# A graph-network kernel: layer 1's wide groups rotate over three row slots, not four

## The chip, the cores and the metric

The kernel runs on one core of one Trainium2 chip. The metric is the device time of one execution in microseconds (us), lower is better. The kernel before took 3185.05 us, the median of three runs (3184.51, 3185.05 and 3190.93).

## What is computed

Two layers of message passing over one graph of 12,500 nodes with 128 float32 features and 212,500 edges, which come sorted by target node (`dst`). The reference, cut to what matters:

```python
def layer0(x, weight, w_comp, h_bias, src, dst, etypes):
    W = einsum('rb,bio->rio', w_comp, weight)      # 16 relations from 8 bases
    h = einsum('ni,rio->rno', x, W)
    return segment_sum(h[etypes, src], dst, 12500) + h_bias
def layer1(feat, W_neigh, W_self, b_self, src, dst):
    deg = maximum(segment_sum(ones, dst, 12500), 1)
    agg = segment_sum(feat[src], dst, 12500)
    return feat @ W_self + b_self + (agg / deg[:, None]) @ W_neigh
x = layernorm(x + layer0(x, ...))                  # called x1 below
x = layernorm(x + layer1(x, ...))
```

The code counts the same two as 1 and 2 (its names are `w1`, `n1` and `w2`, `n2`); "layer 1" below is the first of them, as in the change's title.

## The kernel before, in words

**Tiling.** The edges are cut into chunks of 128, eight chunks (`CPG`) make a group, and there are 208 groups. The last one, 207, has five real chunks. For each chunk GpSimd issues one indirect DMA (L1640, L1644, L1671) which fetches the 128 source rows into one eighth of a slot of the tile `rows`; TensorE multiplies them with a one-hot matrix, and VectorE adds the small result to the target nodes' columns of `acc`.

**Layer 1.** The first 20 groups (`PLAIN`) are narrow: a row is x alone, 512 bytes, and `rows` holds them in eight slots (`SLOTS`), slot g % 8. From group 20 on they are wide: a row of the table `x_x_rows` is x and, beside it, x1 of the same node where that has been laid there already, or zeros, 1024 bytes. A wide slot takes the room of two narrow ones, so `rows` has room for four, and group g uses wide slot g % `WIDE_SLOTS`. For each group TensorE makes layer 1's sums (`sum_half`, L2257), then, from the same slot, layer 2's sums of the sources whose x1 was there (`early_half`, L2269). Its last matmul raises `rows_read`, so `rows_read` is n + 1 when group 20 + n has been read for good.

**Nodes finish as the edges go by.** Every 4.25 groups, one part of 256 nodes (49 parts) is complete: TensorE projects a run of groups (`project`, L2297), VectorE adds (L1909), ScalarE stages (L1701), TensorE transposes (L2225), VectorE and ScalarE normalise, and SyncE stores x1 (L1531 to the wide table for the first 44 parts, counted by `laid1`; L1533 to `x1_rows`, counted by `stored1`).

**What sets the order on GpSimd.** Its program (L1617 to L1674) is one hand-written list. Before group g's gathers it waits until the group that last used the slot has been read: L1621 for narrow groups, L1623 to L1628 for wide ones. Before a half of a wide group it also waits for the table parts that the half may read (L1637). After the last group of layer 1 come the two held groups of layer 2 (`HELD`, j = 0 and 1), whose edges had been left over from narrow groups 18 and 19. They go to narrow slots 0 and 1, that is to wide slot 0, and wait at L1651 for the last group that used wide slot 0, and for parts 45 and 46 to be stored (L1653). Group j = 2 and all behind it read any row of x1 and so wait for the stores of the last two parts (L1662). Then come layer 2's remaining groups, each after the read of the group eight before it (L1663). The lines around the two waits:

```python
1623                            s = g % WIDE_SLOTS
1624                            before = [e for e in range(g) if (e % SLOTS // 2 if narrow(e) else e % WIDE_SLOTS) == s][-1]
...
1628                                pool.wait_ge(rows_read, before - PLAIN + 1)
...
1649                        if j < HELD:
1651                            pool.wait_ge(rows_read, max(e for e in range(groups) if e % WIDE_SLOTS == j // 2) - PLAIN + 1)
...
1660                        if j == HELD:
1661                            for k in (last_part - 1, last_part):
1662                                pool.wait_ge(stored1[k % 2], stores(k))
```

TensorE ends layer 1 with group 207, a projection of that group and the transpose of the last part, and begins layer 2 with `total_late(0)` (L2324) and the sums of j = 0 (L2372). From j = 20 on layer 2's sums are L2379.

Of the kernel before, what the change touches and what calls it, by code (L numbers as in the profile page):

```python
# [31 lines left out]
CPG = 8  # L32
UNROLL = 8
SLOTS = 8
AHEAD = 6
WIDE_SLOTS = 4
TPH = 4
QUAD = TPH * P
SHIFT = 3 * QUAD
# [18 lines left out]
def gnn_kernel(nc, x_in, src, dst, etype, weight, w_comp, h_bias, w_neigh, w_self, b_self, x1_rows, out):  # L58
# [118 lines left out]
    with ctx:  # L177
        def sb(name, shape, dt=F32):
            return ctx.enter_context(nc.sbuf_tensor(name, shape, dt))
# [6 lines left out]
        def sem(name):  # L186
# [8 lines left out]
        xout = sb("xout", [P, 2, TPH, d])  # L195
        rows = sb("rows", [P, SLOTS, CPG, d])
        wide_rows = rows[:, :, :, :].rearrange("p s c f -> p (s c f)").rearrange(
            "p (s c f) -> p s c f", s=WIDE_SLOTS, c=CPG)
        idx = sb("idx", [P, SLOTS, CPG], I32)
        src_t = sb("src_t", [P, chunks + SLOTS * CPG], I32)  # L200
        rel_t = sb("rel_t", [P, chunks])
# [1000 lines left out]
        with nc.If(in_order):  # L1202
# [102 lines left out]
            def narrow(g):  # L1305
                return g < PLAIN

            def slot_rows(g, c):
                return rows[:, g % SLOTS, c, :] if narrow(g) else wide_rows[:, g % WIDE_SLOTS, c, 0:d]

# [150 lines left out]
            with nc.Block(no_gpsimd_drain=True) as block:  # L1461
# [156 lines left out]
                def _(pool):  # L1618
                    for g in range(AHEAD, groups):
                        if narrow(g):  # L1620
                            after(pool, w1.z_done, g - SLOTS + 1)  # L1621
                        else:
                            s = g % WIDE_SLOTS  # L1623
                            before = [e for e in range(g) if (e % SLOTS // 2 if narrow(e) else e % WIDE_SLOTS) == s][-1]
                            if narrow(before):
# [7 lines left out]
                        for c in range(real):  # L1633
# [9 lines left out]
                            else:  # L1643
                                gather = pool.indirect_dma_start(  # L1644
                                    out=wide_rows[:, g % WIDE_SLOTS, c, :], out_offset=None, in_=table,
                                    in_offset=bass.IndirectOffsetOnAxis(ap=src_t[:, k:k + 1], axis=0))
                            gather.then_inc(w1.gathered[g % SLOTS][c // HALF], signal_of(range(real), c))
                    for j in range(late_groups):
                        if j < HELD:
                            pool.wait_ge(held_marked, 1)  # L1650
                            pool.wait_ge(rows_read, max(e for e in range(groups) if e % WIDE_SLOTS == j // 2) - PLAIN + 1)  # L1651
                            for k in (settled - 2, settled - 1):
# [1047 lines left out]
```

## Time and profile before

| | |
|---|---|
| median of three runs | 3185.05 us |
| lowest, highest | 3184.51, 3190.93 us |
| the profiled execution's own time | 3189.88 us |
| its span in the trace | 3188.5 us |
| mean granted TensorE clock | 0.649 |
| indirect DMAs of rows in layer 1 (wide) | 1501 |
| indirect DMAs of rows in layer 2 (held, then all others) | 16, then 839 |

Busy time counts an engine's own instructions. Register, branch and semaphore instructions are not in it. For an indirect DMA the busy time on POOL (GpSimd) is that of issuing it; the landing comes later. Behind a row stands the engine's idle time ahead of it, and what ended that: "issue" where nothing that the profile shows was waited for.

### The profile page before, as it was taken

To read this page: it belongs to the slowest core of one execution; us is meant where nothing else is said; L and a number is where in the kernel's file an instruction comes from. 1 tells how busy PE (TensorE), PEld (TensorE's weight loads), DVE (VectorE), ACT (ScalarE), POOL (GpSimd) and SP (SyncE) were. 2 spreads that over 40 slices of the span, in tenths; PEclk is the share of its full clock that TensorE was granted. 3 is DMA by queue.
4 is the path that set the end of the run, shared out by engine and by line. 5 is a ranking of instruction groups with operands and counts; after the bars stand their busy time and mean duration, and the time that the engine had idled before them with its cause. 6 is when DMAs were issued, how large, how long until landed. Compare 5 with 4: busy or idle time off the path is not lost. (4 is left out here: it accounts for less than half of the span.)

```text
span 3188.5 us, 36471 instructions
## 1 busy us (share of the span) xinstructions
PE 2287.2 (72%) x11654; PEld 2071.9 (65%) x11654; DVE 1557.9 (49%) x4527; ACT 334.1 (10%) x668; POOL 2391.8 (75%) x2528
## 2 busy tenths in 40 slices
PE   2678888888888888888888888864555555555455
PEld 1567777777777778887777887854444444444444
DVE  6453343334333333344333333346677777777345
ACT  2111111111111111111111111100000000000011
POOL 7777777777777777777777777777777777777775
PEclk9876666676666665567666666665565556566576
DMA  4944444444444344444444444332222222222323
GB/s 117 330 129 122 121 121 121 116 122 121 122 125 122 115 122 120 120 120 122 126 120 118 120 122 120 112 83 53 63 68 68 63 63 70 67 73 70 92 80 79
DMA packets 257565, 345.54 MB, mean 108 GB/s; under 512 B 47072, under 2 KB 190021, under 8 KB 257366
## 3 DMA queue, kind: packets, MB, share of 16 engines
q0 software_dynamic: 104528, 263.42, 29.7%
q1 hardware_dynamic: 127398, 66.86, 7.2%
q10 hardware_dynamic: 25440, 12.85, 1.3%
q8 instruction: 95, 1.56, 0.2%
q14 instruction: 104, 0.85, 0.1%
HBM read 311.40 MB, written 44.38 MB: 112 GB/s over the span
## 5 line engine op out<-in xcount | busy, mean ns | idle before, releaser
L1644 POOL DMA_INDIRECT rows<-x_x_rows,src_t x1501 | 1425.3, 950 | 459.7 <-issue 455.7
L2257 PE MATMUL zps<-acc,rows 128*128 128x168 f32 x3322 | 833.0, 415 | 206.5 <-DMA rows<-x_x_rows,src_t 188.4
L2257 PEld LDWEIGHTS zps<-acc,rows 128*128 128x128 f32 x3322 | 715.2, 266 | 238.6 <-DMA rows<-x_x_rows,src_t 122.4
L1671 POOL DMA_INDIRECT rows<-x_rows,picked_mem x695 | 657.6, 946 | 211.8 <-issue 211.5
L2379 PE MATMUL zps<-acc,rows 128*128 128x128 f32 x1390 | 323.2, 406 | 406.9 <-DMA rows<-x_rows,picked_mem 394.0
L2269 PEld LDWEIGHTS yps<-oh,rows 128*128 128x128 f32 x3002 | 579.0, 278 | 0.0
L2379 PEld LDWEIGHTS zps<-acc,rows 128*128 128x128 f32 x1390 | 278.8, 298 | 441.9 <-DMA rows<-x_rows,picked_mem 273.8
L2269 PE MATMUL yps<-oh,rows 128*128 128x21 f32 x3002 | 537.1, 322 | 0.0
L1896 DVE TENSOR_TENSOR acc<-acc,yps 128x42 f32 (+1 forms) x831 | 163.1, 196 | 592.4 <-PE yps L2277 460.4
L1909 DVE TENSOR_TENSOR acc<-acc,tps 128x21 f32 x831 | 146.9, 177 | 540.2 <-PE tps L2297 379.3
L2297 PE MATMUL tps<-acc,picked_mem 128*128 128x336 f32 (+3 forms) x816 | 340.8, 585 | 27.5 <-ACT acc L1723 27.5
L1870 DVE TENSOR_TENSOR acc<-oh,tps 128x1344 f32<-128x1344 f32 x208 | 323.2, 1554 | 29.3 <-PE tps L2244 1.8
L1723 ACT COPY acc<-zps 128x672 f32<-128x672 f32 x208 | 148.4, 714 | 1399.4 <-PE zps L2257 1380.6
L2297 PEld LDWEIGHTS tps<-acc,picked_mem 128*128 128x128 f32 x816 | 199.0, 254 | 146.7 <-issue 90.5
L2109 DVE TENSOR_TENSOR acc<-place_b,tps 128x1024 bf16<-128x1024 bf16 x190 | 230.1, 1211 | 0.0
L2023 DVE TENSOR_TENSOR acc<-acc,zps 128x128 f32 (+1 forms) x448 | 119.9, 268 | 224.7 <-PE zps L2379 139.7
L1671 POOL DMA_INDIRECT rows<-x_rows,src_t x144 | 136.6, 948 | 49.1 <-issue 43.6
L2244 PE MATMUL tps<-wc_blk,acc 128*128 128x64 f32 x416 | 88.8, 386 | 73.3 <-DVE acc L1870 61.4
L2244 PEld LDWEIGHTS tps<-wc_blk,acc 128*128 128x128 f32 x416 | 83.9, 296 | 79.3 <-DVE acc L1870 64.7
L2372 PE MATMUL zps<-oh,rows 128*128 128x21 f32 x320 | 73.8, 380 | 85.5 <-DMA rows<-x_rows,src_t 85.5
L1640 POOL DMA_INDIRECT rows<-in_x_dram,src_t x112 | 107.3, 958 | 34.1 <-issue 33.8
L2372 PEld LDWEIGHTS zps<-oh,rows 128*128 128x128 f32 x320 | 70.2, 325 | 89.7 <-DMA rows<-x_rows,src_t 53.4
(295 smaller groups left out, 1527.6 us busy)
## 6 DMA issues: line engine op xcount, KB each, us to landing
rows<-x_x_rows,src_t POOLq DMA_INDIRECT x1501, 2.7
erep<-in_edge_type_dram SPq DMA_DIRECT2D x207, 64.0 KB
x_x_rows<-zrow ACTq DMA_DIRECT2D x20, 576.0 KB, 3.6
x_x_rows<-in_x_dram SPq DMA_DIRECT2D x20, 576.0 KB
rows<-x_rows,picked_mem POOLq DMA_INDIRECT x695, 2.5
x_rows<-xout SPq DMA_DIRECT2D x49, 128.0 KB
xin<-in_x_dram SPq DMA_DIRECT2D x48, 128.0 KB
out_dram<-xout SPq DMA_DIRECT2D x24, 256.0 KB, 2.4
```

Of the source, the lines that this page charges most:

```text
L1644: gather = pool.indirect_dma_start(out=wide_rows[:, g % WIDE_SLOTS, c, :], out_offset=None, in_=table, in_offset=bass.IndirectOffsetOnAxis ...
L1671: pool.indirect_dma_start(out=rows[:, j % SLOTS, c, :], out_offset=None, in_=x1_rows[0:n_nodes, :], in_offset=bass.IndirectOffsetOnAxis(ap ...
L1723: nc.scalar.copy(zsb[:, kept_at(g)].rearrange("p (h w) b n -> p h (w b n)", h=2), zduos[g % 2]).then_inc(w1.z_copied, 1)
L1870: nc.vector.tensor_tensor(a[:, g % 4], oh1[:, g % 6].unsqueeze(2).to_broadcast([P, CPG, n_bases, SPAN]), wcp[:, m % 2, g % HALF, :].rearra ...
L1896: add = nc.vector.tensor_tensor(target, target, windows_of(g)[:, first:2, c, :], ALU.add)
L1909: add = nc.vector.tensor_tensor(target, target, ybank1[:, y0:y0 + SPAN], ALU.add)
L2109: nc.vector.tensor_tensor(to_lane[:, t % UNROLL], place_b[:, 0, at].unsqueeze(2).to_broadcast([P, CPG, P]), lanes_p.unsqueeze(1).to_broadc ...
L2244: last = nc.tensor.matmul(wcp[:, m % 2, q, :], eoh[:, m % 2, q, :], wc_blk[:, :, :].rearrange("p c b -> p (c b)"), start=True, stop=True)
L2257: last = nc.tensor.matmul(zwins[g % 2][:, c // HALF, c % HALF // 2], slot_rows(g, c), a[:, g % 4, c], start=(c % 2 == 0), stop=(c % 2 == 1 ...
L2269: last = nc.tensor.matmul(windows_of(g)[:, 0, c // 2], wide_rows[:, g % WIDE_SLOTS, c, d:2 * d], oh1[:, g % 6, c], start=(c % 2 == 0), sto ...
L2297: last = nc.tensor.matmul(ybank1[:, y0:y0 + duos * SPAN].rearrange("p (w n) -> p w n", n=SPAN), wb[:, b, :], kept[:, 0:duos, b, :], start= ...
L2379: last = nc.tensor.matmul(sums_of(j, c0, P), rows[:, j % SLOTS, c, :], oh2[:, j % 4, c, :], start=(c == c0), stop=(c == c0 + n - 1))
```

## The change

`WIDE_SLOTS` goes from 4 to 3. The view `wide_rows` keeps its cut into four wide slots (`SLOTS // 2`), of which the fourth is no longer used. All places that take a wide slot or the group before it in that slot (L1309, L1623, L1624, L1645, L1651, L2270) follow the constant. So a wide group waits for the group three before it, not four; group 20 waits for narrow group 13, not 17; and the last group in wide slot 0, for which the held groups wait at L1651, is 207 (207 % 3 = 0), where it was 204 (204 % 4 = 0).

```diff
-WIDE_SLOTS = 4
+WIDE_SLOTS = 3
...
         wide_rows = rows[:, :, :, :].rearrange("p s c f -> p (s c f)").rearrange(
-            "p (s c f) -> p s c f", s=WIDE_SLOTS, c=CPG)
+            "p (s c f) -> p s c f", s=SLOTS // 2, c=CPG)
```

## Rows read from the trace of the kernel before

**Rows 1.** The page's busy times: engine, us, share of the span, instructions

```profile
PE 2287.2 (72%) x11654; PEld 2071.9 (65%) x11654; DVE 1557.9 (49%) x4527; ACT 334.1 (10%) x668; POOL 2391.8 (75%) x2528
```

**Rows 2.** Who POOL waited for, whole span: us in total, times, longest us

```profile
POOL rows L1644 <- issue: 455.7, 1496, 0.3
POOL rows L1671 <- issue: 255.1, 837, 0.3
...
POOL rows L1671 <- DMA x_rows<-xout: 5.5, 1, 5.5
...
POOL rows L1644 <- DMA x_x_rows<-xout: 3.4, 3, 1.8
...
POOL rows L1644 <- PE yps L2269: 0.6, 2, 0.3
```

**Rows 3.** Who PE waited for, 2118 to 3168 us (layer 2)

```profile
PE zps L2379 <- DMA rows<-x_rows,picked_mem: 388.5, 149, 6.2
PE zps L2372 <- DMA rows<-x_rows,src_t: 85.5, 33, 3.5
```

**Rows 4.** The chain that ended last, its first long piece: start, us, what

```profile
3167.39 4.97 DMA rows<-x_rows,picked_mem
```

**Rows 5.** Timeline of POOL, middle of layer 1: start, us, instruction [idle before, releaser]

```profile
1338.99 0.94 POOL L1644 DMA_INDIRECT rows<-x_x_rows,src_t  x1 [1.75 <-DMA x_x_rows<-xout]
1343.98 0.95 POOL L1644 DMA_INDIRECT rows<-x_x_rows,src_t  x1 [0.30 <-PE yps L2269]
...
1384.06 0.95 POOL L1644 DMA_INDIRECT rows<-x_x_rows,src_t  x1 [0.30 <-issue]
```

**Rows 6.** Timeline of PE, middle of layer 1

```profile
1334.27 1.74 PE L2269 MATMUL yps<-oh,rows 128*128 128x21 f32 x8
...
1375.23 1.74 PE L2269 MATMUL yps<-oh,rows 128*128 128x21 f32 x8
```

**Rows 7.** Timeline of POOL, end of layer 1 and start of layer 2

```profile
2067.34 0.95 POOL L1644 DMA_INDIRECT rows<-x_x_rows,src_t  x1 [0.30 <-issue]
...
2092.33 0.95 POOL L1644 DMA_INDIRECT rows<-x_x_rows,src_t  x1 [0.30 <-issue]
2093.58 0.94 POOL L1655 DMA_INDIRECT rows<-x_rows,held_idx  x1 [0.30 <-issue]
...
2112.31 0.94 POOL L1655 DMA_INDIRECT rows<-x_rows,held_idx  x1 [0.31 <-issue]
2118.79 0.94 POOL L1671 DMA_INDIRECT rows<-x_rows,src_t  x1 [5.54 <-DMA x_rows<-xout]
```

**Rows 8.** Timeline of PE, end of layer 1 and start of layer 2

```profile
2061.33 1.74 PE L2269 MATMUL yps<-oh,rows 128*128 128x21 f32 x8
...
2099.94 4.24 PE L2297 MATMUL tps<-acc,picked_mem 128*128 128x168 f32 x16 [5.56 <-ACT acc L1723]
...
2105.96 0.53 PE L2257 MATMUL zps<-acc,rows 128*128 128x168 f32 x2
2106.33 0.29 PE L2269 MATMUL yps<-oh,rows 128*128 128x21 f32 x2
...
2112.38 0.69 PE L2225 MATMUL tps<-ident,stage 128*128 128x128 f32 x2 [3.08 <-ACT stage L1701]
2121.63 0.35 PE L2324 MATMUL yps<-ones_b,late_b 128*112 128x128 bf16 x1 [8.56 <-DVE base_f L2033]
```

**Rows 9.** Timeline of SyncE's issues, same stretch

```profile
2116.19 0.40 SPq L1533 DMA_DIRECT2D x_rows<-xout  x1
```

**Rows 10.** Lines L1644, L1655 and L1671: durations ns min/median/max, first and last start

```profile
L1644 POOL DMA_INDIRECT rows<-x_x_rows,src_t x1501: 940/946/1182, 208.6 to 2092.3; - x188
DMA to landing us min/median/max: 2.7/2.7/3.7
...
L1655 POOL DMA_INDIRECT rows<-x_rows,held_idx x16: 940/944/947, 2093.6 to 2112.3; - x16
...
L1671 POOL DMA_INDIRECT rows<-x_rows,src_t x144: 938/944/1447, 2118.8 to 2298.0; - x144
```

## The prediction, made before the changed kernel was run

> **What bounds the kernel now.** I read the engines' busy times first. POOL is the busiest at 2391.8 us, but that is only 75% of the span, and PE at 72% stands close behind [rows 1]. The shares leave the bound open, so I went on to what POOL waited for. Its idle time is nearly all "issue", 0.3 us before each indirect DMA: 1496 of layer 1's 1501 wide gathers, and 837 of layer 2's 839 [rows 2]. A gather costs 0.946 us plus those 0.30 us [rows 2, 10], 1.25 us from start to start, a group of eight 10 us. Real waits are few: 3.4 us for table parts in layer 1 and 5.5 us once, at the switch to layer 2 [rows 2]. From the first wide gather at 208.6 us to the end POOL issues almost without a break, and PE waits for its rows in layer 2: 388.5 us in 149 waits at L2379, 85.5 us in 33 at L2372 [rows 3]. The chain that ended last has as its first long piece the last gather on its way, from 3167.39 us for 4.97 us [rows 4]. So POOL's list of gathers bounds the kernel, in both layers. A new stall on POOL ahead of layer 2's gathers moves the end by its whole length; a later PE, DVE or ACT does nothing until POOL waits for it.
>
> The change adds no instruction and takes none away. It changes for which group POOL waits, in three places.
>
> **1. Into the wide groups.** Group 20 waits for group 13, not 17; groups 21 and 22 wait for 17 and 19, earlier groups than PE's newest. These waits are no tighter than the old ones, so they can't cost; and they can't gain more than the 0.6 us in two waits that is all L1644 ever waited for PE, each no longer than the usual 0.3 [rows 2]. Worth 0.
>
> **2. The steady rotation.** Group g now waits until PE has read g - 3. I compare POOL's first gather of g with the end of PE's L2269 of g - 3 in the unchanged timeline; while that difference stays above zero the new wait is already over. Near the end, group 205 starts at 2067.34 us and PE has read 202 at 2061.33 + 1.74 = 2063.07, a slack of 4.3 us [rows 7, 8]. That is the smallest of the 185 differences. In the middle PE falls behind too: group 133 starts at 1343.98, group 130 is read at 1334.27 + 1.74 = 1336.01, slack 8.0; group 137 at 1384.06 against 1375.23 + 1.74 = 1376.97, slack 7.1 [rows 5, 6]. In that same episode POOL already idles 1.75 us, 1.45 above the usual 0.30, for a table part (the gather at 1338.99 us [rows 5]). That wait comes from the same late PE and binds with 7 to 8 us of slot slack left, so in the middle it holds POOL back before a three-slot wait does. At the end no table part is waited for any more (the last of the 44 is asked for in group 191), and the 4.3 us are unguarded. Worth 0 here; if PE is some us later in another execution a slot wait appears. At the end that costs nothing either, by step 3: there PE's own end sets the time. I keep 0 to +3 us (two waits like the 1.45 above).
>
> What hides the removed slot is thus PE's distance of under three groups. The Trainium skill ("Trainium Kernel Development and Optimization", Best Practices) says to double-buffer so that DMA and compute overlap; by it three slots are one more than needed and the sum would be 0, no change. The trace agrees for the rotation, by the 4.3 us. It isn't all the change does.
>
> **3. The held groups.** This is the step that I expect to cost. Before, the 16 held gathers wait for group 204 and follow the last gather of 207 without a pause: 2092.33, then 2093.58, with 0.30 us of "issue" [rows 7]. Now wide slot 0 is last used by group 207 itself, of which the last rows have only just been asked for. PE has read 207 at 2106.33 + 0.29 = 2106.62 us [rows 8]; that is 13 us behind POOL, since PE is catching up and loses 5.56 us to a late copy of ACT before the projection at 2099.94 [rows 8]. So:
> - First held gather: 2106.62 + 0.30 = 2106.9 us, against 2093.58. POOL stands for 13.3 us.
> - The 16 gathers take (2112.31 - 2093.58) / 15 = 1.249 us each, 20.0 us in all [rows 7]. Next one possible: 2126.9 us.
> - Before, the gathers were done at 2112.31 + 0.94 = 2113.25, and POOL then idled 5.54 us for the store of the last part, so j = 2 began at 2118.79 [rows 7]. That store is issued at 2116.19 [rows 9] and hangs on PE, ACT and DVE behind group 207 (the transpose at 2112.38 [rows 8]), none of which waits for a held gather. It is then over before 2126.9 and costs nothing.
> - Loss: 2126.9 - 2118.79 = **8.1 us**. Of the 13.3 us, 5.2 are paid out of the old wait (5.54 less the 0.30 of issue).
>
> It hardly depends on when PE ends. If PE reads 207 later or earlier by a few us, old and new start of j = 2 both move with it, as the old one is set by the store 12.17 us after that read (2118.79 - 2106.62). Only once the store would be in time for the end of the old gathers (read of 207 before 2106.62 - 5.24 = 2101.4 us) does the loss shrink by 1 us per us. Lower end: rows of the last gather land 2.7 us after 2092.33 [rows 10], PE needs 0.53 + 0.29 us for them [rows 8], so the read ends at 2095.9 at the earliest, j = 2 starts at 2095.9 + 0.3 + 20.0 = 2116.2 against 2113.6: +2.6 us. Upper end: +8.1, and one long gather of step 4, 8.6.
>
> **4. Behind it.** Nobody waits for held rows early: PE takes up j = 0 only after 2121.63, where it had been waiting 8.56 us for DVE's L2033 [rows 8]. j = 0 is landed by then, j = 1 some us later; PE then follows POOL as before. The moved gathers now run at 2107 to 2127 us, beside other DVE work. In the old place they took 940 to 947 ns each, and the 144 gathers that come next, beside the DVE work of layer 2's start, have the same median, 944 ns, with a longest of 1447 [rows 10]. So I take 0, and 0.5 us, one such gather, as the bound; a gain is excluded, as the shortest is 938.
>
> **Sum.** 0 + 0 + 8.1 + 0: the profiled execution, 3189.88 us (span 3188.5 and 1.4 around it), would become 3198.0. It is itself 4.8 us above the median of 3185.05, and nothing in the loss hangs on that difference, so I put the 8.1 on the median: 3193.1 us, +0.25%.
>
> **Rivals.**
> - *PE isn't late at the end* (the mildest case of step 3). If PE reads 207 before 2099.6 us, the loss is under 6.3 us; at the floor it is 2.6 and the time 3187.6, under 0.2% and not to be told from no change. For it: the clock differs between executions. Against it: PE's late end is mostly ACT's late copy and the projection behind it, 2099.94 + 4.24, which don't go away with the clock. 9%.
> - *No stall that counts, not slower*. The mechanism: POOL's 13.3 us stand but layer 2 catches up, because its pace is set by PE or DVE and POOL had run ahead into its eight slots. Price 0, time 3185.1. It decides if PE's lag there exceeds the 8.1 us. Against it: 182 waits of PE for rows, 474 us [rows 3], and no wait of POOL for a slot in layer 2 [rows 2]. It is also what the rule on double buffering gives. 7%.
> - *Slot waits in layer 1 as well*. PE's lag differs by execution, and the slack of 4.3 or 7.1 us runs out in the middle of the layer. Two or three waits of 1 to 1.8 us (the table's wait is the nearest row [rows 5]) add 3 to 5 us: 3196 to 3198. 9%.
> - *The change doesn't act*, because some index still counts four slots: every use takes the constant, and the view alone keeps four. 1%.
>
> **The numbers.** The forecast, 3193.1, has 74%. A measurement of this kernel can tell 0.2%, 6.4 us, from no change; the three runs of before spread over as much. The range goes from the floor of step 3, 3185.05 + 2.6 = 3187.6, to the highest run with the loss, 3190.93 + 8.1 = 3199.0. Slower by over 0.2%: the forecast and the slot waits, 83%, less about 10 for a scatter that hides 8.1 under 6.4, 73%. Within 0.2%: the mild case, the catching up and no action, 17%, and most of that 10, less what scatters out: 25%. Faster: 2%, scatter alone, as nothing on POOL's path gets earlier.
>
> **What would show it.** In the changed profile: POOL's first L1655 with an idle time of about 13 us ended by PE's L2269, 16 gathers in 20 us, then L1671 at once with 0.30 of issue in place of 5.54 for the store; layer 2 from there on as long as before, 1048.6 us from its first L1671 to its last; layer 1's L1644 with the same few waits as before, all 1501 within 1884 us. I'd be wrong if L1644 showed waits for L2269 of more than 0.3 us (step 2), if L1671 still waited for the store (step 3), or if layer 2's stretch came out shorter (step 4).

## The result, and the profile after

The changed kernel takes **3193.26 us** (median of 14 runs, 3191.35 to 3200.51) where the kernel before takes 3185.86 us (median of 14 runs, 3182.78 to 3192.57 and one of 3232.99). The ratio is 1.0023, 95% interval 1.0015 to 1.0031: slower by 7.4 us. The forecast was 3193.1.

The page's busy times are those of before [rows 1] to within 10 us:

```profile
PE 2277.4 (71%) x11654; PEld 2063.7 (65%) x11654; DVE 1557.7 (49%) x4527; ACT 334.1 (10%) x668; POOL 2392.7 (75%) x2528
```

Who POOL waited for in the changed kernel, whole span (in all, times, longest us):

```profile
POOL rows L1644 <- issue: 456.0, 1497, 0.3
POOL rows L1671 <- issue: 255.4, 838, 0.3
...
POOL rows L1655 <- issue: 12.4, 16, 7.8
POOL rows L1644 <- DMA x_x_rows<-xout: 3.9, 4, 1.4
```

Against [rows 2] one entry is new and one is gone. L1655, the held gathers, now has one idle stretch of 7.8 us; L1671's wait of 5.5 us for the store is no longer there. L1644 has no wait for L2269 at all, so the rotation over three slots never held POOL up.

The timeline of POOL at the switch of layers, which answers to [rows 7]:

```profile
2093.81 0.95 POOL L1644 DMA_INDIRECT rows<-x_x_rows,src_t  x1 [0.30 <-issue]
2102.56 0.94 POOL L1655 DMA_INDIRECT rows<-x_rows,held_idx  x1 [7.80 <-issue]
...
2121.30 0.94 POOL L1655 DMA_INDIRECT rows<-x_rows,held_idx  x1 [0.30 <-issue]
2122.55 0.95 POOL L1671 DMA_INDIRECT rows<-x_rows,src_t  x1 [0.30 <-issue]
```

PE, which answers to [rows 8]:

```profile
2095.20 4.13 PE L2297 MATMUL tps<-acc,picked_mem 128*128 128x168 f32 x16 [2.13 <-ACT acc L1723]
...
2101.49 0.29 PE L2269 MATMUL yps<-oh,rows 128*128 128x21 f32 x2
```

and SyncE, which answers to [rows 9]:

```profile
2111.35 0.40 SPq L1533 DMA_DIRECT2D x_rows<-xout  x1
```

PE has read group 207 at 2101.49 + 0.29 = 2101.78 us, and POOL starts the held gathers 0.78 us later. The profile calls the idle time "issue" and names no releaser. That it is the wait of L1651 for group 207 is read from the program and from this distance; the experiments below put the wait in and take it out by itself. The store of the last part, on which j = 2 hung before, is issued at 2111.35 and by the 2.6 us of before (2116.19 to 2118.79 [rows 7, 9]) would let POOL go at 2113.95. It is long over at 2122.55.

**Where the time went.** From the last wide gather to the first of j = 2 it is 28.74 us (2093.81 to 2122.55), against 26.46 in the profiled execution of before [rows 7]. Those 26.46 hold 5.24 us of waiting for the store: 17 gathers in a row take only 17 x 1.249 = 21.2 us. With the changed kernel's own PE and store the old wait would have given 21.2 us, j = 2 at 2115.0, later than the 2113.95 of the store. So the change costs 7.5 us in this execution. The profiled executions lie only 3.7 us apart (3188.5 and 3192.2 in span), as that of before was 4.0 us above the median of its 14 runs and that of the changed kernel 0.4 above its own. Without its 5.24 us of waiting for the store the profiled execution of before would have taken 3184.64 us, which is near that median. It fits that most executions of before have no such wait, but none of them was traced.

### The profile page after: what moved, and what is told of

It is laid out like the page before. It is cut to its first block, busy times and chain, and to the rows that moved or that the text cites. A ratio compares the mean times of both kernels' runs of the same rounds, so it can differ in the third digit from the quotient of the medians.

```text
span 3192.2 us, 36471 instructions
## 1 busy us (share of the span) xinstructions
PE 2277.4 (71%) x11654; PEld 2063.7 (65%) x11654; DVE 1557.7 (49%) x4527; ACT 334.1 (10%) x668; POOL 2392.7 (75%) x2528
## 4 chain that ended last, share of the span: by engine, by line
POOL 70%; issue 23%; PE 4%; DVE 1%; DMA 1%; DVEq 0%; ACT 0%; POOLq 0%; ACTq 0%; SPq 0%
POOL rows L1644 41%; POOL rows L1671 24%; POOL rows L1640 3%; PE zps L2257 2%; POOL rows L563 1%; PE tps L2297 1%; PE yps L2269 1%; POOL rows L1655 0%; DVE acc L1909 0%; PE zps L2379 0%; PE tps L2244 0%; DMA rows<-x_rows,picked_mem 0%; DVE acc L1870 0%; DMA rows<-x_x_rows,src_t 0%; DVEq L1909 0%
## 5 line engine op out<-in xcount | busy, mean ns | idle before, releaser
L1644 POOL DMA_INDIRECT rows<-x_x_rows,src_t x1501 | 1426.0, 950 | 459.9 <-issue 456.0
L1671 POOL DMA_INDIRECT rows<-x_rows,picked_mem x695 | 657.3, 946 | 211.8 <-issue 211.5
L2379 PE MATMUL zps<-acc,rows 128*128 128x128 f32 x1390 | 326.3, 409 | 398.8 <-DMA rows<-x_rows,picked_mem 377.4
L2269 PEld LDWEIGHTS yps<-oh,rows 128*128 128x128 f32 x3002 | 570.2, 274 | 0.0
L2379 PEld LDWEIGHTS zps<-acc,rows 128*128 128x128 f32 x1390 | 282.2, 301 | 433.7 <-DMA rows<-x_rows,picked_mem 277.1
L2269 PE MATMUL yps<-oh,rows 128*128 128x21 f32 x3002 | 528.4, 319 | 0.0
L2297 PE MATMUL tps<-acc,picked_mem 128*128 128x336 f32 (+3 forms) x816 | 331.2, 572 | 24.2 <-ACT acc L1723 24.1
L1671 POOL DMA_INDIRECT rows<-x_rows,src_t x144 | 136.4, 947 | 43.9 <-issue 43.9
L2372 PE MATMUL zps<-oh,rows 128*128 128x21 f32 x320 | 75.0, 383 | 91.6 <-DMA rows<-x_rows,src_t 89.5
L2372 PEld LDWEIGHTS zps<-oh,rows 128*128 128x128 f32 x320 | 71.1, 328 | 96.2 <-DMA rows<-x_rows,src_t 54.9
```

Of the source, the lines that this page charges most:

```text
L1644: gather = pool.indirect_dma_start(out=wide_rows[:, g % WIDE_SLOTS, c, :], out_offset=None, in_=table, in_offset=bass.IndirectOffsetOnAxis ...
L1671: pool.indirect_dma_start(out=rows[:, j % SLOTS, c, :], out_offset=None, in_=x1_rows[0:n_nodes, :], in_offset=bass.IndirectOffsetOnAxis(ap ...
L2269: last = nc.tensor.matmul(windows_of(g)[:, 0, c // 2], wide_rows[:, g % WIDE_SLOTS, c, d:2 * d], oh1[:, g % 6, c], start=(c % 2 == 0), sto ...
L2297: last = nc.tensor.matmul(ybank1[:, y0:y0 + duos * SPAN].rearrange("p (w n) -> p w n", n=SPAN), wb[:, b, :], kept[:, 0:duos, b, :], start= ...
L2379: last = nc.tensor.matmul(sums_of(j, c0, P), rows[:, j % SLOTS, c, :], oh2[:, j % 4, c, :], start=(c == c0), stop=(c == c0 + n - 1))
```

## The experiments

Three theories were set against each other. A: all the loss is the held groups' wait, and the rotation is free. B: the shorter rotation itself costs. C: layer 2 makes a delay good. Seven kernels were run, three of them more than once, since something unforeseen turned up: on the chips of the first eight (numbers 9 and 3) the kernel before takes 4364 us, on that of the last four (number 0) 3185 to 3188 us, like the runs of the result. Each ratio is against the kernel before on the same chip. The expectations call 9 and 3 the slow chips. I take chip 0 first, which is like that of the result.

### The held groups without the wait, three slots

Layer 2's groups are moved round by six narrow slots, so the held ones land in narrow slots 6 and 7, which three wide slots leave free, and L1651 is dropped:

```diff
+HELD_AT = 6
...
-                            pool.wait_ge(rows_read, max(e for e in range(groups) if e % WIDE_SLOTS == j // 2) - PLAIN + 1)
...
-                                    out=rows[:, j, c, :], out_offset=None, in_=x1_rows[0:settled * PART, :],
+                                    out=rows[:, (j + HELD_AT) % SLOTS, c, :], out_offset=None, in_=x1_rows[0:settled * PART, :],
...
-                                out=rows[:, j % SLOTS, c, :], out_offset=None, in_=x1_rows[0:n_nodes, :],
+                                out=rows[:, (j + HELD_AT) % SLOTS, c, :], out_offset=None, in_=x1_rows[0:n_nodes, :],
```

(and the same index in L2372 and L2379).

> Three wide slots, the held groups in narrow slots 6 and 7 without a wait for rows_read, a third time, in the hope of a chip on which before takes 3185 us, as in the last two runs. There my theory (all the loss is the held groups' wait) gives the time of before, within 3 us; the rival (the rotation over three slots costs) gives +7 us, as in the changed kernel. On a slow chip it says nothing new: 3975 us.

Measured: 3185.22 us (12 runs) against 3187.64 (22 runs), ratio 0.9993 (0.9984 to 1.0003). The same as before. The new constant moves the lines down by one, so its wide gathers are L1645. POOL at the switch:

```profile
2094.94 0.95 POOL L1645 DMA_INDIRECT rows<-x_x_rows,src_t  x1 [0.30 <-issue]
2096.19 0.94 POOL L1655 DMA_INDIRECT rows<-x_rows,held_idx  x1 [0.30 <-issue]
...
2114.92 0.94 POOL L1655 DMA_INDIRECT rows<-x_rows,held_idx  x1 [0.30 <-issue]
2116.16 0.94 POOL L1671 DMA_INDIRECT rows<-x_rows,src_t  x1 [0.30 <-issue]
```

2094.94 to 2116.16 is 21.2 us, the bare 17 gathers. And what L1645 waited for in this kernel:

```profile
  issue: 454.8, 1493
  DMA x_x_rows<-xout: 6.6, 5
  PE yps L2269: 0.9, 3
```

Three waits named PE, of 0.3 us each, which is the usual gap. The five waits for table parts hold 5.1 us above it, against 2.5 in three before [rows 2]; they are no slot waits. B falls on this chip: three slots without the held wait cost nothing.

### The held wait alone, four slots

```diff
-                            pool.wait_ge(rows_read, max(e for e in range(groups) if e % WIDE_SLOTS == j // 2) - PLAIN + 1)
+                            pool.wait_ge(rows_read, groups - PLAIN)
```

> Four wide slots, the held groups wait for group 207 to be read, a third time. Where before takes 3185 us my theory gives +7 to +8 us, with POOL idle 7 to 14 us before the first held gather and 0.30 us before j = 2; the rival gives 0. On a slow chip: 4370 us again.

Measured: 3194.85 us (11 runs) against 3187.64, ratio 1.0027 (1.0018 to 1.0035), 7.2 us more. The wait alone makes all of the change's loss. POOL and, behind it, PE at the switch:

```profile
2090.53 0.94 POOL L1644 DMA_INDIRECT rows<-x_x_rows,src_t  x1 [0.30 <-issue]
2101.20 0.94 POOL L1655 DMA_INDIRECT rows<-x_rows,held_idx  x1 [9.73 <-issue]
...
2121.18 0.94 POOL L1671 DMA_INDIRECT rows<-x_rows,src_t  x1 [0.30 <-issue]
```

```profile
2100.13 0.29 PE L2269 MATMUL yps<-oh,rows 128*128 128x21 f32 x2
```

From the read of 207 (2100.42 us) to the first held gather it is 0.78 us again, and 19.98 us more to j = 2.

### A lead of two groups

Four slots, and POOL waits in addition until PE has read g - 2:

```diff
                                 pool.wait_ge(rows_read, before - PLAIN + 1)
+                            if g - 2 >= PLAIN:
+                                pool.wait_ge(rows_read, g - 2 - PLAIN + 1)
```

> Four wide slots as in the kernel before, with one wait more: a wide group g also waits until PE has read g - 2. Only POOL's lead over PE is that of two slots; the slots, the addresses and the held groups' wait are those of before. On the chips of the first eight runs (before 4364 us, PE's slow stretches): if the gain of fewer slots there comes from the shorter lead, about 3820 us, as with two slots. If it comes from where the rows lie, 4364 us. Where before takes 3185 us: 4 to 16 us more than before, from waits for L2269 while PE lags.

Measured on chip 0: 3202.01 us (4 runs) against 3185.29 (7 runs), ratio 1.0052 (1.0035 to 1.0069), 16.7 us more, just over my range of 4 to 16. What its wide gathers (L1646 here, by the two lines added) waited for:

```profile
L1646 POOL DMA_INDIRECT rows<-x_x_rows,src_t x1501: 940/946/1201, 209.2 to 2108.9; - x188
its engine sat idle before it (us, times) until:
  issue: 446.7, 1456
  PE yps L2271: 29.1, 45
```

The 45 waits for PE make 29.1 us, 15.6 above the usual 0.3 each; only ten of them are longer than 0.8 us. Layer 1's gathers take 1899.7 us, where those of before take 1883.7 [rows 10]. So the edge lies between three and two: a lead of three groups is free, one of two costs 16 us. The smallest slack over three slots, 4.3 us [rows 7, 8], says so beforehand: with one group of 10 us less it would be -5.7.

### A pause at each group

Four slots, and POOL waits before each wide group for its own last gathers to land:

```diff
+                        if g > PLAIN:
+                            for h in range(2):
+                                pool.wait_ge(w1.gathered[(g - 1) % SLOTS][h], ((g - 1) // SLOTS + 1) * 16 * HALF)
```

> Four wide slots and the full lead of four groups, but POOL waits before each wide group until its own last group of gathers has landed, a pause of about 2 us a group that doesn't depend on PE. On the slow chips PE's slow stretches end 3 to 6 us after POOL stops issuing. If POOL's unbroken issue is what keeps PE slow, regular pauses of 2 us shorten the stretches and the kernel gets faster than before's 4364 us, to 3850 to 4150, in spite of 187 pauses. If only the lead over PE counts, PE stays as slow and the pauses are lost or swallowed: 4350 to 4700 us. Where before takes 3185 us: about 187 x 1.7 = 320 us more than before.

It ran on chip 0, so it only shows the price there: 3629.88 us (4 runs), ratio 1.1393 (1.1374 to 1.1412), 444.6 us more, against 320 that I had expected. Its wide gathers waited:

```profile
  DMA rows<-x_x_rows,src_t: 483.2, 186
```

2.60 us each, 2.30 above the usual, and not the 1.7 that I had put. 187 x 2.3 = 430. The time rises by all of POOL's stalls again, and by some 15 us more. What it was made for, chips 9 and 3, stayed untried.

### The same kernels on chips 9 and 3

The changed kernel itself:

> The changed kernel itself, beside variants that part its two effects. The first four variants ran on a chip (number 9 in the results) where the kernel before takes 4363.8 us, not 3185, and where PE stood still for about 1 ms in all with nothing that it waited for. Where before takes about 3185 us again, I expect +7 to +8 us for this kernel. Where before takes about 4360 us again, the variants with fewer slots were 9 and 12% faster there, so I expect this one 8 to 9% faster.

3976.14 us (6 runs) against 4364.82 (17 runs), ratio 0.9125 (0.9089 to 0.9162). There it is **faster by 389 us**.

The two kernels that part A and B, each run on chip 9 and again on chip 3:

> Three wide slots as in the change, but layer 2's groups are moved round by six narrow slots, so the held groups land in narrow slots 6 and 7, which no wide group uses now, and their wait for rows_read falls away. My theory (the loss is all in the held groups' wait, the rotation over three is free): as the kernel before, within 0.1%; POOL's last wide gather is followed by the first held one after 0.30 us. Rival (the shorter rotation itself costs, by slot waits in layer 1): it stays slower by about 7 us, as the changed kernel, and L1644 shows waits for PE's L2269 well over 0.3 us.

> Three wide slots, the held groups in narrow slots 6 and 7 and without a wait for rows_read, a second time. Where before takes about 3185 us: my theory gives no difference to before (within 0.1%), the rival, that the shorter rotation costs, gives +7 us as in the changed kernel. On the slow chip: as a1_changed less 8 us at most.

3979.32 us against 4363.77, ratio 0.9125 (0.9101 to 0.9150), and 3972.38 against 4364.82, ratio 0.9117 (0.9080 to 0.9155). Not the time of before, as I had expected of the first, but within 4 us that of the changed kernel.

> Four wide slots as before, and only the held groups' wait is that of the change: for group 207 to be read. My theory: +7 to +8 us against the kernel before, as the changed kernel, with one idle stretch of 7 to 13 us on POOL before the first held gather and none before layer 2's j = 2. Rival (the rotation costs): within 2 us of the kernel before.

> Four wide slots, the held groups wait for group 207 to be read, a second time. Where before takes about 3185 us: my theory gives +7 to +8 us, the rival 0. On the slow chip it was +5 us of 4364, inside the scatter, and I expect that again.

4369.22 us, ratio 1.0018 (0.9996 to 1.0041), and 4375.86, ratio 1.0032 (1.0005 to 1.0059): 5 and 11 us more, of runs that scatter over 40 to 50. The first had been expected 7 to 8 us slower; on these chips so small a loss can't be told from none.

Two wide slots and the free held groups (`WIDE_SLOTS = 2`):

> The kernel e1_held_free with two wide slots, so a wide group waits for the group two before it, and the held groups wait for none. In the trace of before, 21 of 186 groups would start up to 5.7 us too early for that, in three stretches where PE lags (groups 60 to 72, 128 to 141, 196 to 207). My theory: real waits for L2269 appear in those stretches alone, a few us each time a stretch begins, less of them once POOL has fallen back; layer 1's last wide gather comes 8 to 20 us later and the time rises by 4 to 16 us, as the last stretch is free. Rival (POOL's lead over PE is only needed where it has one, PE's lag is made good): under 3 us.

> Two wide slots and the held groups free of the wait, a second time. Where before takes about 3185 us: real waits for L2269 in the stretches where PE lags, layer 1's last wide gather 8 to 20 us later, the time up by 4 to 16 us; the rival says under 3 us. On the slow chip: 12% faster again.

3827.25 us, ratio 0.8778 (0.8754 to 0.8802), and 3818.84, ratio 0.8755 (0.8725 to 0.8784). Faster still, by 12%, where I had expected 4 to 16 us more of the first. It wasn't run on chip 0; by the lead of two above I estimate that it would lose some 16 us there.

Eight more gathers in layer 2, whose rows nothing reads:

```diff
+                        if j == 3:
+                            for c in range(CPG):
+                                pool.indirect_dma_start(
+                                    out=rows[:, (7 + HELD_AT) % SLOTS, c, :], out_offset=None, in_=x1_rows[0:n_nodes, :],
+                                    in_offset=bass.IndirectOffsetOnAxis(ap=src_t[:, c:c + 1], axis=0)
+                                ).then_inc(w1.gathered[0][0], 16)
```

> The kernel e1_held_free with eight further gathers of rows on POOL, behind those of layer 2's j = 2, into a slot that is idle then; nothing reads them. It asks whether POOL's list bounds layer 2 throughout. My theory: the end moves by all of 8 x 1.249 = 10.0 us against e1_held_free. Rival (layer 2 catches a delay up, since PE or DVE set its pace): less than 5 us.

(At j = 7 it also waits for these eight to have landed.) 3997.69 us (5 runs), 18.4 more than the kernel without them, where 10.0 had been expected. Of the two traces, layer 2's first and last L1671 say more, as layer 1 differed too. Without them, then with them (L1679 there):

```profile
L1671 POOL DMA_INDIRECT rows<-x_rows,picked_mem x695: 942/947/1287, 2918.7 to 3930.8; - x174
L1671 POOL DMA_INDIRECT rows<-x_rows,src_t x144: 942/947/1057, 2712.8 to 2914.4; - x144
```

```profile
L1679 POOL DMA_INDIRECT rows<-x_rows,picked_mem x695: 942/947/1347, 2943.8 to 3957.8; - x174
L1679 POOL DMA_INDIRECT rows<-x_rows,src_t x144: 942/947/1154, 2726.9 to 2939.7; - x144
```

1218.0 us without, 1230.9 with: 12.9 for 10.0 of gathers, in one trace of each. Nothing was made good, which speaks against C even where layer 2 isn't bound by POOL alone. Where the rest of the 18.4 comes from is open.

### What differs on chips 9 and 3

The single gather is hardly slower: the wide ones have a median of 949 ns with four slots on chip 9, and 946 before [rows 10]. PE stands still with nothing that it waits for, and DVE and ACT wait longer in turn. Of the kernel with the held wait alone (four slots) on chip 9, four lines with much idle time, two of PE, one of DVE and one of ACT:

```profile
L2257 PE MATMUL zps<-acc,rows 128*128 128x168 f32 x3322 | 828.4, 404 | 283.5 <-issue 237.1
L2269 PE MATMUL yps<-oh,rows 128*128 128x21 f32 x3002 | 519.1, 307 | 217.5 <-issue 217.1
L1896 DVE TENSOR_TENSOR acc<-acc,yps 128x42 f32 (+1 forms) x831 | 163.4, 197 | 1062.4 <-remote 796.0
L1723 ACT COPY acc<-zps 128x672 f32<-128x672 f32 x208 | 147.8, 714 | 2349.7 <-remote 1583.6
```

("remote" is the profile's word where the update that released an engine isn't in the records.) Its timeline, PE first and then POOL:

```profile
1355.09 0.28 PEld L2244 LDWEIGHTS tps<-wc_blk,acc 128*128 128x128 f32 x1 [1.62 <-issue]
...
1371.22 0.29 PEld L2257 LDWEIGHTS zps<-acc,rows 128*128 128x128 f32 x1 [2.51 <-issue]
1372.62 0.44 PE L2257 MATMUL zps<-acc,rows 128*128 128x168 f32 x1 [2.36 <-issue]
1374.02 0.29 PEld L2257 LDWEIGHTS zps<-acc,rows 128*128 128x128 f32 x1 [2.51 <-issue]
1374.72 0.44 PE L2257 MATMUL zps<-acc,rows 128*128 128x168 f32 x1 [1.66 <-issue]
...
1378.22 1.26 PE L2269 MATMUL yps<-oh,rows 128*128 128x21 f32 x5 [0.30 <-issue]
1379.31 2.59 PE L2257 MATMUL zps<-acc,rows 128*128 128x168 f32 x8
```

```profile
1372.20 0.95 POOL L1644 DMA_INDIRECT rows<-x_x_rows,src_t  x1 [0.31 <-issue]
1378.59 0.95 POOL L1644 DMA_INDIRECT rows<-x_x_rows,src_t  x1 [5.44 <-remote]
```

From 1355 us on PE takes one to two instructions in 1.4 us, for 23 us on end, and is back at its pace at 1378.22, 5 us after POOL has stopped at 1373.15. Such stretches return all through its layer 1. So PE reads a group late, the parts are late, and POOL runs its four groups ahead into the wait for the table:

```profile
POOL rows L1644 <- DMA x_x_rows<-xout: 723.8, 40, 25.1
```

In the changed kernel on chip 3 that wait is far shorter:

```profile
POOL rows L1644 <- DMA x_x_rows<-xout: 259.4, 42, 22.6
...
POOL rows L1644 <- PE yps L2269: 81.9, 23, 8.2
```

A reading that fits all of this is that PE gets its instructions late while POOL issues gathers without a break. POOL's stops give it air, and a shorter lead makes the stops come sooner. The traces agree with it in two ways. In layer 1 of the trace with four slots, PE's idle times of over 0.35 us with nothing waited for come to 502 us; POOL stops there for over 3 us 78 times, and none of the 502 us lies later than 5.5 us after a stop and before POOL's next gather, though the stops hold 532 us from there on. And this idle time falls with the slots: 502 us with four, 351 with three (the changed kernel, chip 3), 193 with two (chip 9), and none in the profile of before. The switch of layers fits as well. In the changed kernel on chip 3, POOL (first fence) rests for 22.24 us, and PE (second) has read 207 at 2686.34, 22.4 us after the last wide gather:

```profile
2663.93 0.95 POOL L1644 DMA_INDIRECT rows<-x_x_rows,src_t  x1 [0.30 <-issue]
2687.12 0.95 POOL L1655 DMA_INDIRECT rows<-x_rows,held_idx  x1 [22.24 <-issue]
...
2707.16 0.95 POOL L1671 DMA_INDIRECT rows<-x_rows,src_t  x1 [0.30 <-issue]
```

```profile
2686.05 0.29 PE L2269 MATMUL yps<-oh,rows 128*128 128x21 f32 x2
```

With the held groups free of the wait, on the same chip, POOL goes on issuing and PE needs 38.0 us (2660.53 to 2698.51), so that the store is late by more than the wait had cost (from the last wide gather to j = 2 it is 49.8 us, and 43.2 in the changed kernel):

```profile
2660.53 0.95 POOL L1645 DMA_INDIRECT rows<-x_x_rows,src_t  x1 [0.30 <-issue]
2661.78 0.95 POOL L1655 DMA_INDIRECT rows<-x_rows,held_idx  x1 [0.30 <-issue]
...
2710.29 0.94 POOL L1671 DMA_INDIRECT rows<-x_rows,src_t  x1 [28.84 <-DMA x_rows<-xout]
```

```profile
2698.22 0.29 PE L2269 MATMUL yps<-oh,rows 128*128 128x21 f32 x2
```

That POOL's issuing is the cause is argued, not shown: POOL's stops and PE's lag depend on each other in all these kernels, and issuing a gather isn't parted from moving its rows. The kernel that would have told it, with pauses that don't depend on PE, ran on chip 0 alone. So did the lead of two in four slots, so whether fewer slots gain by the shorter lead or by where the rows lie is untested as well. Why two chips take 4364 us at all is open too.

**A version that holds on both kinds.** Three slots with the held groups in narrow slots 6 and 7 take the time of before on chip 0 (0.9993) and 8.8% less on chips 9 and 3 (0.9125 and 0.9117). It beats the changed kernel by 0.3% where before takes 3185 us (0.9993 and 1.0023, each against before) and equals it on chip 3 (0.9117 and 0.9125), the only one of the slow chips on which the changed kernel was run.

## Why the prediction was right

- **The bound.** POOL's list, in both layers. Layer 2 from first to last L1671 took 1048.6 us before, 1048.2 after (2122.6 to 3170.7), 1048.6 without the held wait (2116.2 to 3164.8): starts that lie up to 6.4 us apart are carried to the end whole.
- **Step 1, the first wide groups: 0.** No wait there. One premise was wrong without effect: group 22's wait is tighter than before, for 19 and not 13 (22 % 4 = 2, the place of narrow groups 12 and 13). In the trace of before group 19 was read 16 us ahead of group 22's first gather.
- **Step 2, the rotation: 0.** Right where before takes 3185 us: 0.9993 with three slots and no held wait, and no wait for L2269 in the changed kernel. The smallest slack over three slots, 4.3 us in the trace that I had read, was 6.2 us in the changed kernel's. The sign that I named against myself, L1644 waiting for L2269 over 0.3 us, showed only with a lead of two. The rule of the Trainium skill on double-buffering ("Trainium Kernel Development and Optimization", Best Practices) gave 0 for the whole change; the rotation bears it out for three slots, and the lead of two, by its 16.7 us, doesn't.
- **Step 3, the held groups: 8.1.** The mechanism holds, and the wait alone gives 7.2 us by medians. The terms came out otherwise than put. PE read 207 at 8.0 us behind the last wide gather, not 14.3, so POOL's idle stretch was 7.8 us, 7.5 above the usual, and not 13.3 above it; but then the old wait for the store would have been nothing, and not 5.2. The step had said where that begins: the old wait is gone, and the loss shrinks by 1 us per us, once PE reads 207 less than 14.29 - 5.24 = 9.05 us behind the gather. At 8.0 that leaves 7.0. The first held gather followed the read by 0.78 us, not 0.30, which adds 0.5: 7.5 for the changed kernel's profile. In the kernel with the wait alone PE read 207 at 9.9 us behind (2100.42 against 2090.53), so there the old wait would still have been for the store (issued 9.6 us after the read, 2.6 us until POOL goes on, 2112.6). Its j = 2 started at 2121.18, a loss of 8.6: the 8.1 and the same 0.5.
- **The luck in it.** That the time met the forecast within 0.2 us is partly chance. The stall and the refund from the old wait were both over 5 us too large and cancelled, as the step said that they would; and the loss by medians, 7.4, lay 0.7 below the 8.1, while the median of before over 14 runs lay 0.8 above the 3185.05 that I had added to.
- **The sign of step 3.** I wrote that the profile would name PE's L2269 as the releaser. It said "issue", and the idle time was 7.8 us and not about 13.
- **Step 4: 0.** The 16 moved gathers took 20.0 us, 2102.56 to 2122.55, as before.
- **The rivals.** The first, that PE isn't late at the end, came close. It asked for a read of 207 less than 7.3 us behind the last wide gather (2099.6 against 2092.33), and the changed kernel's profile has 8.0; without the 0.5 of the later start its loss is 7.0, where the rival said under 6.3. The second, that layer 2 makes it good, falls by the 1048 us above. The third, slot waits in layer 1, showed nothing.
- **What it left out.** All of it holds for a chip like that of the profile read. Nothing in that profile spoke of engines that stall by themselves, and on such chips the same change gives 9% the other way (chip 3).

## What to carry to other kernels

When a buffer constant changes, look for every wait that is worked out from it. On a chip like that of the profile the steady rotation had 4 us of slack over three slots and was free; the loss came from one hand-off at the end, where the last user of the slot had changed from group 204 to 207. If an engine's queue is the bound, count slack as its own next start less the other side's finish, group by group, and count a wait at a hand-off against the wait that already stands behind it. And a slot given up is room gained: moving the next stage's first loads there took the loss back.

## What the runs showed of the hardware

- The same program took 3185 to 3188 us on one chip and 4364 us on two others, with wide gathers of a median of 946 and 949 ns. On the latter PE had stretches of one to two instructions per 1.4 us; the one shown ended 5 us after POOL had stopped issuing, and none in layer 1 of that trace went on for more than 5.5 us after a stop.
- On those chips fewer slots were faster: 4365, 3976 and 3819 us for four, three and two on chip 3 (the last with the held groups free of the wait, which by itself changed little: 3972 for three).
- At the switch of layers the first held gather, which waits for a count that PE raises, started 0.78 us after the end of PE's last L2269 matmul, as the profile gives it, in the three traces shown (2102.56, 2101.20 and 2687.12 us). It isn't one constant: the ten long waits with a lead of two in layer 1 show 0.75, and with two slots on chip 3 one gather (at 342.55 us) follows PE's matmul by 0.28.
- To wait for one's own last gather before the next cost 2.3 us above the usual gap each time, 186 times over.
